# Identity matmuls on TensorE at four places around two stage boundaries of a two-layer transformer kernel

## The reference, cut to what matters

```
h = layernorm(x) * (1 + ca) + sa
x = x + ga * attention0(h)      # 32 heads of 16; for each token, heads against heads
h = layernorm(x) * (1 + cb) + sb
x = x + gb * ffn0(h)            # base matrix, plus top-2 of 16 low-rank experts
... second layer, with its own six vectors:
x = x + ga * attention1(layernorm(x) * (1 + ca) + sa)   # latent attention, 32 heads
x = x + gb * ffn1(layernorm(x) * (1 + cb) + sb)
```

## Time and profile before

| | us |
|---|---|
| three runs | 901.45, 903.19, 907.17 |
| median | 903.19 |
| profiled execution, its own time | 899.29 |
| its span in the trace | 897.1 |
| PE busy | 816.5 (91%) |
| DVE busy | 681.6 (76%) |
| POOL busy | 538.9 (60%) |
| ACT busy | 535.0 (60%) |
| mean granted PE clock | 0.967 of 2.4 GHz |

### The profile page before, as it was taken

The page is one execution under the profiler, slowest core; times in us unless marked ns, Lnnn a source line. Parts: engine busy times, 40 slices in busy tenths (PEclk is TensorE's granted clock), DMA queues, the critical chain, the costliest instruction groups (busy, mean ns, idle before and its releaser), DMA issues.

```text
span 897.1 us, 15066 instructions
## 1 busy us (share of the span) xinstructions
PE 816.5 (91%) x4560; PEld 537.7 (60%) x4560; DVE 681.6 (76%) x1322; ACT 535.0 (60%) x1158; POOL 538.9 (60%) x481
## 2 busy tenths in 40 slices
PE   3899994899995997899999999999999999999997
PEld 1588873667774874565656565655656556565543
DVE  4768896835443477989989898889998889898652
ACT  5668874733323775666666666665666666665522
POOL 3333432021222237998989888887888888897213
PEclk8899997899997998999999999999999999999999
DMA  8630000494424442666666666665566766565511
GB/s 330 216 122 2 1 2 3 133 245 152 128 68 152 124 130 50 162 159 155 155 150 156 152 155 152 157 155 139 141 155 183 187 150 156 145 159 138 133 33 70
DMA packets 91459, 120.07 MB, mean 134 GB/s; under 512 B 30386, under 2 KB 41650, under 8 KB 91380
## 3 DMA queue, kind: packets, MB, share of 16 engines
q1 hardware_dynamic: 66804, 85.54, 34.5%
q10 hardware_dynamic: 24576, 33.59, 15.2%
HBM read 41.45 MB, written 2.10 MB: 49 GB/s over the span
## 4 chain that ended last, share of the span: by engine, by line
PE 42%; DVE 9%; issue 6%; ACTq 2%; ACT 2%; POOL 1%; DMA 0%; POOLq 0%; DVEq 0%; SPq 0%
PE bank L1558 10%; PE bank L1545 6%; PE bank L1546 4%; PE bank L1547 4%; PE bank L1572 4%; PE bank L1574 3%; PE bank L1573 3%; PE bank L1616 3%; DVE blk L1664 3%; ACTq L1507 2%; DVE cT_lo L1736 2%; DVE stage_a L1200 1%; DVE nmax L1648 1%; DVE stage_a L1203 1%; PE bank L1183 1%
## 5 line engine op out<-in xcount | busy, mean ns | idle before, releaser
L1648 DVE TENSOR_REDUCE nmax<-bank 128x1 f32<-128x512 f32 x256 | 174.0, 680 | 45.0 <-PE bank L1547 43.9
L1798 ACT ACTIVATE prob<-bank,nmax 128x512 f32<-128x512 f32 x172 | 118.1, 687 | 100.1 <-DVE nmax L1648 88.2
L1886 POOL TENSOR_TENSOR prob<-prob,rinv 128x512 f32<-128x512 f32 x129 | 132.6, 1042 | 31.7 <-DVE rinv L1656 29.5
L1545 PE MATMUL bank<-xk_hi,q_hi 128*128 128x512 f32 x256 | 112.9, 441 | 15.7 <-ACT prob L1798 8.8
L1664 DVE STREAM_TRANSPOSE blk<-prob 128x512 f32<-128x512 f32 x172 | 120.0, 698 | 6.5 <-ACT prob L1840 5.1
L1545 PEld LDWEIGHTS bank<-xk_hi,q_hi 128*128 128x128 f32 x256 | 48.5, 189 | 93.8 <-issue 53.8
L1546 PE MATMUL bank<-xk_lo,q_hi 128*128 128x512 f32 x256 | 101.6, 397 | 0.0
L1547 PE MATMUL bank<-xk_hi,q_lo 128*128 128x512 f32 x256 | 100.7, 393 | 0.0
L1217 POOL TENSOR_TENSOR q_lo<-stage_a,q_hi 128x512 fp32r<-128x512 f32 x64 | 82.2, 1285 | 25.4 <-ACT q_hi L1208 25.2
L1798 ACT ACTIVATE stage_a<-bank,nmax 128x512 f32<-128x512 f32 x84 | 57.7, 687 | 48.7 <-DVE nmax L1648 43.4
L1213 POOL TENSOR_TENSOR stage_a<-stage_a 128x512 f32<-128x512 f32 x64 | 82.8, 1294 | 4.8 <-DMA stage_a<-stage_a 4.8
(11 more groups left out here) (251 smaller groups left out, 1934.2 us busy)
## 6 DMA issues: line engine op xcount, KB each, us to landing
pT<-blk SPq DMA_DIRECT2D x256, 64.0 KB, 2.1
pT<-blk ACTq DMA_DIRECT2D x256, 64.0 KB, 2.1
raw_e<-blk SPq DMA_DIRECT2D x256, 64.0 KB, 2.1
raw_e<-blk ACTq DMA_DIRECT2D x256, 64.0 KB, 2.1
raw_e<-in_wo SPq DMA_DIRECT2D x16, 512.0 KB, 3.9
stage_a<-stage_a SPq DMA_DIRECT2D x128, 64.0 KB, 2.1
raw_e<-in_wmod SPq DMA_DIRECT2D x6, 1024.0 KB, 7.7
stage_a<-in_wmod SPq DMA_DIRECT2D x12, 512.0 KB, 4.7
```

The source lines that it names most:

```text
L1545: pe.matmul(sbk, q_hi[:, u % 2, q], xk_hi[:, 2, ks], start=True, stop=False)
L1648: dve.tensor_reduce(nmax[:, s % RING:s % RING + 1], s_bank[s % 2][:, :], AX.X, ALU.max, negate=True).then_inc(max_done, 1)
L1798: act.activation(prob[s % RING], s_bank[s % 2][:, :], ACT.Exp, bias=nmax[:, s % RING:s % RING + 1], accum_out=rsum[:, s % RING:s % RING + ...
L1886: pool.tensor_tensor(prob[s % RING], prob[s % RING], bc(rinv[:, s % RING:s % RING + 1], [P, S]), ALU.mult).then_inc(norm_pool, 1)
```

## The change

A helper `keep_busy` multiplies the 128x128 unit matrix `ident` by itself, in float32, into a bank of PSUM, `count` times. It is called at four places on PE: 46 times at the end of block A, behind a wait for the last `sub_done` (so that DVE has read the scores' bank); 18 times at the start of block B, ahead of the first transposes; 36 times at the end of block B; and 18 times at the start of block C, ahead of its first transposes. Nobody reads the results. Nothing else is changed.

```diff
@@ -121,6 +121,10 @@
+        def keep_busy(pe, ps, count):
+            for _ in range(count):
+                pe.matmul(ps[:, 0:P], ident[:, :], ident[:, :], start=True, stop=True)
@@ -757,6 +761,8 @@
                         if t == 0:
                             columns(1)
                             rows(4)
+                    pe.wait_ge(sub_done, 2 * TILES)
+                    keep_busy(pe, s_bank[0], 46)
@@ -1097,6 +1103,7 @@
+                    keep_busy(pe, m_bank, 18)
                     nrm.pe_xT(pe, 0, pT)
                     pe.wait_ge(wide_set, 5)
                     for t in range(TILES + 1):
@@ -1125,6 +1132,7 @@
                         if 1 <= t <= 6:
                             rows(t - 1)
+                    keep_busy(pe, z_bank[0], 36)
@@ -1372,6 +1380,7 @@
+                        keep_busy(pe, gate_bank, 18)
                         nrm.pe_xT(pe, 0, pT)
                         pe.wait_ge(split2_lo, wc_base + KC)
```

## The result

Ten runs of the changed kernel have a median of 911.43 us (908.85 to 914.71), ten of the kernel before one of 902.97 us (897.72 to 908.47). The ratio is 1.0077, 95% interval 1.0048 to 1.0106: slower by 7.0 us, between 4.3 and 9.6. The profiled execution took 911.5 us with a span of 909.3 us, 12.2 us more than the one before.

What follows compares the result with a forecast made beforehand. PE sets the pace inside the blocks, not at the boundaries, where barriers also wait for PE. Terms 6.0 + 0.0 + 3.9 + 1.2 - 1.0 = +10.1 us (8.0 to 12.4) on a 903.2 us median gave 913.3 us, range 908 to 918.

Steps and rivals of the forecast that it cites:

- The barrier waits for PE's matmuls: At the ends of blocks A and B, PE's drain lasts until its last matmul; slack ahead of the barriers 5.9 and 4.3 us.
- The price of a call: Each added float32 128x128 matmul leaves two records and costs 0.223 us at 2.4 GHz, so no group fits its gap.
- The rival of one record a call: All four groups: a call costs 0.112 us or less, the fills nearly fit, time does not rise, 902 us; chance 6%.
- End of block A: 46 calls from 149.7, first at the lower clock, move the barrier from 155.8 to 161.8: plus 6.0 us, 5.3 to 6.7.
- Start of block B: 18 calls delay ACT by 1.2 us, but the higher clock gives it back: zero, from -0.2 to +0.3 us.
- End of block B: 36 calls at 2.4 GHz move the barrier from 284.0 to 287.9: plus 3.9 us, between 3.8 and 4.1.
- Start of block C: 18 calls delay ACT's first activation behind the barrier, with nothing behind to take it up: plus 1.2 us.
- What the clock gives in block C: First products and couple up to 2.0 us faster if the clock holds, else nothing: minus 1.0 us, between -2.0 and 0.
- How soon the clock rises: Dense PE work raises the clock after 3.4 to 4.4 us; at block A's end at 152.7, between 151.3 and 154.1.
- rival 2: Block B: PE's saving ahead of the router's maximum counts, at most 1.8 us, so +8.3 us, 911.5 us; chance 8%.
- rival 3: All four groups: the fills neither hold nor raise the clock, about +33 us, 936 us; chance 4%.
- I set the same difference on the median: Whole kernel: the +10.1 us of the profiled execution, 899.3 to 909.4, added to the runs' median 903.2, giving 913.3 us.

Runs made afterwards that it cites:

- the doubled ends: Changed kernel with 92 and 72 calls at the ends of blocks A and B instead of 46 and 36; ratio 1.0299 to the kernel before, +27.1 us.
- the transposes: Changed kernel, all four groups with their counts, each call a transpose of the unit matrix instead of a matmul; ratio 0.9986 to the kernel before.
- the fitted kernel: Changed kernel with its four groups cut to 19, 9, 18 and 9 calls to fit their gaps; ratio 1.0009 to the kernel before.
- the fitted kernels: Counts 19, 9, 18, 9 plus 11 calls in block C (0.9969), also 5 ahead of block B's first couple (0.9934), then 6 moved (0.9942); ratios to kernel before.
- the 5 calls alone: Kernel before with only 5 calls added ahead of the first couple in block B; ratio 0.9966, medians 902.50 and 902.96 us.

## Why the prediction was right, and where it was not

- **The barrier waits for PE's matmuls.** Right: PE's drains end after DVE's, by 6.1 and 3.9 us.
- **The price of a call.** 0.223 us expected; 0.220 and 0.222 us by the doubled ends. The rival of one record a call is refuted by the counts, and its consequence was seen with the transposes.
- **End of block A, +6.0 (5.3 to 6.7).** Measured 14.1 - 8.0 = 6.1, 6.0 in the second profile. The clock rose at 154.5, 4.8 us after the last context's start at 149.72, where I took 4.9 (152.7 - 147.85).
- **Start of block B, 0.** The exponential is at 8.3 us behind the barrier, as before (8.25 against 8.30), which was the prediction. The couple is 1.0 us late in the first profile and 0.3 in the second; the load was issued in time (19.1 us behind the barrier in both kernels) and landed later. I had not counted a spread of the load.
- **End of block B, +3.9.** Measured 8.7 - 4.8 = 3.9.
- **Start of block C, +1.2 from the calls.** Measured 8.3 - 7.2 = 1.1.
- **What the clock gives in block C, -1.0 (-2.0 to 0).** Measured 6.5 - 7.2 = -0.7, -0.5 in the second profile. It was neither of my two outcomes (the clock holds, or nothing is gained): the clock fell, but came back 3.0 us after the first product instead of 4.4. The size of my -1.0 is therefore a middle between two cases that did not come. The whole of it, 7.2 - 5.1 = 2.1, came with calls in the pause in three profiles of three, and without them in one of six, the doubled ends.
- **How soon the clock rises.** I took 3.4 to 4.4 us of dense work. That gave the right moment in block A. But in block C it took 9.4 us with the transposes, and in block B of the fitted kernel the clock was down for 13.7 us with PE busy for nearly all of it.
- **More clock gain in block B (rival 2).** The mechanism was partly there: the fitted groups brought the router's exponential 1.25 us forward, since in the kernel before ACT's table load was through 1.21 us ahead of the exponential, at 162.94, and only DVE's maximum held it up, so that my argument against this rival was wrong; but in the changed kernel nothing of it arrived, and no more than 1.0 us of it did where the fitted kernels had no fall (23.1 against 24.1 us to the couple).
- **Calls that do not raise the clock (rival 3).** Refuted by the clock's row at 154.7.

In the profile the sum is 6.1 + 1.0 + 3.9 + 1.1 - 0.7 = +11.4 us against 10.1 forecast. In the runs it is +7.0 us by the ratio (4.3 to 9.6) and +8.5 us by the medians, 911.4 against 913.3 forecast. So the sign held, and the median lies in the range of 908 to 918. But that range had 1.5 us of margin on each side: by the ratio the 7.0 us lie below the sum's own bounds of 8.0 to 12.4, the interval ends just short of my 10.1, and the chance of 0.67 for slower by over 1% went to a case that did not come: 0.77%. (The sum behind that chance, 0.82 x 0.8 + 0.04, is 0.70 and not 0.69.) The step that failed is the one from one profiled execution to the runs, "I set the same difference on the median". It takes the changed stretch of the kernel before as 190.2 us in every run. All its profiles say so, yet both comparisons of the changed kernel (10 and 11 runs) give a difference of 7.0 and 7.1 us by the ratio, 4 less than the 11.4 and 10.9 us of its two profiles' stretches. If the clock fell now and then at the first couple in the kernel before, its runs would be longer than its profiles; the 5 calls alone, at 0.9966, speak for that. No profile of it caught such a fall. Another reading is that the changed kernel is often faster than its two profiles: had its clock held in block C, as with the doubled ends, its stretch would be 1.3 us shorter. That alone is not 4 us. Which of the two it is, or what else, stays open; in ten of the eleven comparisons here the ratio gives less time than the stretch, by up to 5.8 us.

## What to carry to other kernels

Work that only keeps an engine's clock up must fit into the gap it fills: count the records that a call leaves, take the spacing of their starts and not their mean duration, and remember that a block's end waits for all of it. Filling is worth something only where that engine's speed sets the next stage, and then it should reach up to the work that profits; here 11 calls in the two small pauses ahead of block C's products gave 2.1 us there in each of three profiles. The 118 of the change, which left these pauses open, gave 0.7 and 0.5; with the pauses open the clock held only once in six profiles. Compare stretches between landmarks over several profiles before a difference of spans is explained: untouched code varied by 7 us here. And do not carry a stretch of two or three profiles over to the runs as it stands: whether the clock falls in a pause differs from execution to execution.

## What the runs showed of the hardware

- Float32 transposes of 128 columns, issued one behind the other, raised PE's clock in block A as matmuls did, in the one profile that has them (0.50 up to 154.9, 1.00 after). The Trainium skill ("TensorE: Matmul & The Clock Gate", Part 4: PE-mode transpose) says that they do not count as busy in the same way; this trace does not agree: with 2.8 us of them behind the context matmuls the clock rose, and with those matmuls alone it did not.
- PE's drain lasts until its queued matmuls are done: behind the added ones it took 2.17 us each time (161.4 to 163.6, 294.4 to 296.6, and with the fitted counts 153.3 to 155.5), where the kernel before had 0.95 and 4.07 us.
- The same pause does not always end the upper level: in the 8.3 us from barrier B to block C's products the clock fell at 304.7 in the changed kernel and stayed at 1.00 with the doubled ends.
- A load issued 1.2 us earlier landed no earlier in the fitted kernel (24.5 us behind the barrier, against 24.1); issued 1.1 to 1.3 us earlier, it landed 0.9 to 1.1 us earlier in three others (23.1 to 23.3).
